# Set-up and projections of the first attention as one unrolled block: composed norms, and the next group's rows and turns during the present group

## The reference

```
def _ln(x, g, b):
    m = jnp.mean(x, -1, keepdims=True)
    v = jnp.var(x, -1, keepdims=True)
    return (x - m) * jax.lax.rsqrt(v + 1e-05) * g + b
...
x = _ln(xx, ln1_g, ln1_b)
...
xn = _ln(x, lnx_g, lnx_b)
yn = _ln(y, lny_g, lny_b)
q = jnp.einsum('bsc,hcd->bhsd', xn, wq)
k = jnp.einsum('btc,hcd->bhtd', yn, wk)
v = jnp.einsum('btc,hcd->bhtd', yn, wv)
```

## Time and profile before

| | |
|---|---|
| time before, median of 3 executions | 2344.16 us (2343.84 to 2350.32) |
| the profiled execution's own time | 2343.02 us |
| its span, first to last instruction | 2341.2 us |
| PE busy, share of the span | 1960.3 us, 84% |
| DVE busy | 1316.7 us, 56% |
| ACT busy | 1011.8 us, 43% |
| POOL busy | 533.9 us, 23% |
| mean granted clock of PE, as a share of full speed | 0.941 |

### The profile page before, as it was taken

How to read it: one execution, slowest core, us unless ns; L and a number is a source line. 1 busy time by engine, 2 the same in 40 slices (tenths; PEclk the granted TensorE clock), 3 DMA queues, 4 the chain that set the end, 5 groups by cost and what they waited for, 6 DMA issues and landing times. The chain is left out here.

```text
span 2341.2 us, 32500 instructions
## 1 busy us (share of the span) xinstructions
PE 1960.3 (84%) x11836; PEld 1237.5 (53%) x11836; DVE 1316.7 (56%) x2301; ACT 1011.8 (43%) x2111; POOL 533.9 (23%) x909
## 2 busy tenths in 40 slices
PE   3778888888799797996999989979999898973695
PEld 1335555555566465663565655535656455442594
DVE  3548888888633597233666632246666343876212
ACT  1238888888622342221656621126565111531121
POOL 2102222222333300332222211022222111131321
PEclk9889999999999899997999999989999999986797
DMA  2243111110000100003000000030000000035395
GB/s 68 72 133 112 40 38 41 40 37 2 1 1 1 54 1 1 1 0 94 1 1 1 1 1 1 0 106 1 1 1 1 1 0 14 1 122 134 115 307 156
DMA packets 99133, 99.60 MB, mean 43 GB/s; under 512 B 33740, under 2 KB 83232, under 8 KB 98848
## 3 DMA queue, kind: packets, MB, share of 16 engines
q1 hardware_dynamic: 95904, 93.21, 13.0%
q0 software_dynamic: 3072, 4.34, 1.0%
HBM read 80.60 MB, written 16.92 MB: 42 GB/s over the span
## 5 line engine op out<-in xcount | busy, mean ns | idle before, releaser
L515 DVE TENSOR_REDUCE negmax<-sps 128x1 f32<-128x1024 f32 x256 | 308.0, 1214 | 21.5 <-PE sps L466 20.8
L559 ACT ACTIVATE prob<-sps,negmax 128x1024 f32<-128x1024 f32 x256 | 286.2, 1118 | 9.2 <-DVE negmax L515 6.5
L475 PE MATMUL sps<-ident,prob 128*128 128x128 f32 x1152 | 178.9, 283 | 55.8 <-ACT prob L559 54.7
L475 PEld LDWEIGHTS sps<-ident,prob 128*128 128x128 f32 x1152 | 131.7, 142 | 144.7 <-ACT prob L559 129.4
L466 PE MATMUL sps<-ks,qs 128*128 128x512 f16 x512 | 162.9, 390 | 22.1 <-DVE ores L535 18.8
L604 POOL TENSOR_TENSOR probT<-probT,after 128x128 f32<-128x128 f32 x256 | 116.5, 455 | 276.8 <-DVE probT L523 192.3
L568 ACT COPY probT<-sps 128x512 f32<-128x512 f32 (+1 forms) x192 | 101.6, 529 | 18.8 <-PE sps L475 18.8
L1313 POOL TENSOR_TENSOR la1qs<-la1qn,la1sin 128x256 f32<-128x256 f32 x64 | 60.3, 971 | 196.7 <-DVE la1qn L1390 196.7
L1313 POOL TENSOR_TENSOR la0qs<-la0qn,la0sin 128x256 f32<-128x256 f32 x64 | 60.3, 971 | 195.6 <-DVE la0qn L1390 195.6
L523 DVE COPY probT<-sps 128x512 f32<-128x512 f32 (+3 forms) x192 | 91.7, 478 | 1.5 <-PE sps L475 1.5
L491 PE MATMUL sps<-probT,vres 128*32 128x128 f32 x2304 | 81.6, 277 | 8.5 <-POOL probT L604 5.7
(11 more groups left out here) (450 smaller groups left out, 4249.2 us busy)
## 6 DMA issues: line engine op xcount, KB each, us to landing
w1e<-in_fc_T SPq DMA_DIRECT2D x16, 1024.0 KB, 5.7
w2e<-in_fc_T SPq DMA_DIRECT2D x16, 1024.0 KB, 8.4
qs<-q_parts SPq DMA_DIRECT2D x128, 64.0 KB, 1.9
ks<-k_parts SPq DMA_DIRECT2D x128, 64.0 KB, 1.9
q_parts<-parts SPq DMA_DIRECT2D x8, 512.0 KB
k_parts<-parts SPq DMA_DIRECT2D x8, 512.0 KB
token_rows<-r_row SPq DMA_DIRECT2D x4, 544.0 KB
mixed<-r_zero SPq DMA_DIRECT2D x1, 2056.0 KB, 10.6
```

What stands on the lines that cost most here:

```text
L475: mm = pe.transpose(slots[n % 4][:, at * P:(at + 1) * P], prob[:, n % 3, t * P:(t + 1) * P], ident[:])
L515: dve.tensor_reduce(negmax[:, n % 4:n % 4 + 1], slots[n % 4][:], X, ALU.max, negate=True).then_inc(s.max_done, 1)
L559: act.activation(prob[:, n % 3, :], slots[n % 4][:], ACT.Exp, bias=negmax[:, n % 4:n % 4 + 1], accum_out=rowsum[:, tile % 2, n % QUAD:n % ...
```

## The change

Both blocks become one, with no loop in it and with more semaphores, so that each step waits for just what it needs.

- The first two norms are composed. With m and v the mean and variance of a row, the doubly normed row is (x - m) / sqrt(v (1 + eps) + eps^2). DVE takes the statistics of x once, writes (x - m) * ln1g (`centre`, L268) and, with the inverse root, times it plus ln1b (`place_x0`, L281) straight to `x0res`. POOL is left with the constants.
- DVE's norm of group g+1 is cut into eight pieces, `norm_piece(g + 1, n)`, one behind each of the eight remainders `low_part(g, n)` (L343) of group g. The third norm is among them.
- PE turns group g+1 (L426) behind the tenth tile of group g; ACT makes its xT and yT there, in a second pair of buffers (the second yT lies in the place of a weight of a later block).
- PE begins a group's q tiles once xT is there (two ACT instructions instead of four), and k and v with yT.
- The copy of v goes from DVE to ACT (L392).
- SP loads the first quarter of x, then `ln1g` and `ln1b`, the four small vectors, the weights one semaphore each, then the rest of x and the gates; it sends q after tile 3 and k after tile 7. DVE begins when the first quarter of x and the two rows are there.
- tanh of the gates (L414) is ACT's last instruction in the block.

The core of the diff, with the old scheduling functions of DVE, ACT and PE left out:

```diff
-        def ln_vector(e, s, n, src, dst, out=None):
...
             with nc.Block() as block:
                 @block.sync
                 def _(sp):
+                    load_x(0)
+                    sp.dma_start(ln1g[:], rows(io["L0_xattn_ln1_g"])).then_inc(s.rows_in, 16)
+                    sp.dma_start(ln1b[:], rows(io["L0_xattn_ln1_b"])).then_inc(s.rows_in, 16)
...
+                    for g in range(1, G):
+                        load_x(g)
...
                     for g in range(G):
                         b, gg = g // (G // B), g % (G // B)
-
-                        sp.wait_ge(s.hi_done, 1 + g * 8 + 8)
-                        sp.wait_ge(s.proj_free_dve, 1 + g * 8 + 8)
                         for t, dst in enumerate((q_parts, k_parts)):
+                            sp.wait_ge(s.hi_done, g * 8 + t * 4 + 4)
+                            sp.wait_ge(s.lo_done, g * 8 + t * 4 + 4)
...
+                    def norm_piece(g, n):
+                        if n == 0:
+                            stats_x(g)
+                        elif n == 1:
+                            moments_x(g)
+                            centre(g, 0)
+                            centre(g, 1)
+                        elif n == 2:
+                            centre(g, 2)
+                            centre(g, 3)
+                            inverse_x(g)
+                        elif n == 3:
+                            place_x0(g, 0)
+                            place_x0(g, 1)
+                        elif n == 4:
+                            place_x0(g, 2)
+                            place_x0(g, 3)
+                        elif n == 5:
+                            stats_x0(g)
+                        elif n == 6:
+                            moments_x0(g)
+                        else:
+                            inverse_x0(g)
+                            normed(g)
...
+                    dve.wait_ge(s.rows_in, 32)
+                    for n in range(8):
+                        norm_piece(0, n)
+                    for g in range(G):
                         for n in range(8):
...
+                            low_part(g, n)
+                            if g + 1 < G:
+                                norm_piece(g + 1, n)
...
+                    for g in range(G):
+                        for n in range(8):
+                            high_part(g, n)
+                            if n == 2 and g + 1 < G:
+                                root_x(g + 1)
+                        if g + 1 < G:
+                            root_x0(g + 1)
+                        value(g, 8)
+                        value(g, 9)
+                        if g + 1 < G:
+                            affine(g + 1)
+                        value(g, 10)
+                        value(g, 11)
+                    act.wait_ge(s.gates_in, 32)
+                    act.activation(gate[:], gate[:], ACT.Tanh).then_inc(s.tanh_done, 1)
...
+                    turn(0)
+                    for g in range(G):
+                        for n in range(12):
+                            project(g, n)
+                            if n == 9 and g + 1 < G:
+                                turn(g + 1)
```

325 lines of the change are left out of this document (169 added, 156 removed).

## The result

| | before | after |
|---|---|---|
| median of 4 executions each, same chip | 2344.55 us (2343.84 to 2350.32) | 2286.23 us (2284.53 to 2287.81) |
| ratio, 95% interval | | 0.9747 (0.9735 to 0.9759) |
| the profiled execution's own time | 2343.02 us | 2286.99 us |
| its span | 2341.2 us | 2285.2 us |
| first matmul of the attention | 164.31 us | 108.28 us |

The change saves 58.3 us between the medians, where 50.4 were forecast. The expected things happened: no group boundary with a wait, a start 22.65 us earlier, and PE's clock up from the end of the first q tiles to the block's end. What was wrong are sizes, nearly all to the same side.

A forecast was written before the change was run, and what follows sets the result against it. PE was taken to bound the block before the attention, losing time to start, boundaries and clock. Savings 19.4 + 26.2 + 5.7 less 0.6 and 0.3 lost gave 50.4 us, a median of 2293.8, range 2288 to 2302.

The forecast's parts named there:

- What bounds the stretch: Block before the attention: PE's matmuls fill 82.3 of 161 us; the rest is start, boundaries and clock.
- the first load: Before DVE's first instruction: quarter of x and two rows there at 8.3 us instead of 13.01, saving 4.7.
- The chain to the first projection: From DVE's first instruction to PE's first projection: 13.2 us instead of 27.86.
- The boundaries: Between PE's groups: only transposes stay, three boundaries cost 3.0 us and not 29.2, saving 26.2.
- a late `h`: At the group boundaries: DVE's `h` level with PE, no margin; 0.2 us a boundary, 0.6 lost.
- The rival of a late DVE: DVE late at every group boundary, 2.2 us each: 2300, or 2307 if the clock falls too; chance 0.17.
- The clock: PE's q tiles: clock stays up after the first group's ramp; 2.7 of 8.4 us lost remain, 5.7 saved.
- the clock stayed low: Rival: PE's unbroken run of 192 f32 instructions stays at the low clock, 79.6 us later, 2373; chance 0.02.
- The end: Block's end: ACT is last, 3.6 us from PE's end to the attention's first matmul, 0.3 lost.
- The table switch: Rival: switching costs a drain, 1.4 us more at the first root and at the block's end, 2296.6; chance 0.08.
- The stated range: For the median: own range 2289 to 2298 us, widened to 2288 to 2302 for drain and late DVE.
- The clock behind the barrier: At the attention's start: clock's state uncertain by 2 us either way, as a ramp cost 1.5 to 2.7.

The follow-up runs named there:

- e3: Changed kernel with the third norm (pieces 5 to 7), the turn and xT of the next group behind the present group's last tile; ratio 0.9879.
- e5: Kernel before the change with only the first two norms composed into one; ratio 0.9983, attention starts at 160.58 us.
- e4: Changed kernel with the four small vectors' transfers issued ahead of ln1g and ln1b; ratio 0.9773, attention starts at 111.52 us.
- e7: Changed kernel with three more DVE statistics instructions, results unread, for each of a group's four tiles; ratio 0.9823.
- e10: Changed kernel with tanh of the gates moved behind ACT's third high part of the last group; ratio 0.9743, PE's stop 1.56 us.
- e6: Changed kernel with four extra ACT instructions ahead of tanh, stretching PE's stop at the block's end to 5.03 us; ratio 0.9760.
- e13: Changed kernel with one small ACT copy ahead of tanh's table load; one execution, PE's stop 3.24 us, first heads 12.77 us.
- e16: Changed kernel with one small ACT copy ahead of tanh's table load, repeated; one execution, PE's stop 3.24 us, first heads 12.75 us.
- e17: Changed kernel with three small ACT copies ahead of tanh's table load; one execution, PE's stop 3.58 us, first heads 12.74 us.
- e1: Changed kernel with PE turning the next group behind the twelfth tile instead of the tenth; ratio 0.9766, attention starts at 114.97 us.
- e2: Changed kernel with one buffer each for xT and yT, the turns still behind the tenth tile; ratio 0.9779.
- e18: Changed kernel with the turn behind the twelfth tile, run again; one execution, attention starts at 114.53 us, first heads 12.11 us.
- e8: Changed kernel with 72 transposes of the identity on PE ahead of the first turn; ratio 0.9754, attention starts at 108.25 us.
- e12: Changed kernel with early tanh, finer start, and 96 identity transposes on PE ahead of the first turn and 12 behind it; ratio 0.9726.
- e15: Changed kernel with early tanh and finer start, without identity transposes; ratio 0.9732, attention starts at 104.23 us.

## Why the prediction was wrong, point by point

**What bounds the stretch** was right. e3 brings the boundary back by its two waits and the clock; e5, which takes a norm and nothing else, gains at the start alone.

**The step that failed** is the first load. It was put as "The two rows, 2 x 131 KB spread to 128 partitions, ran at 93 GB/s in their window, thus 2.8 us more, 7.4", which with 0.9 for the signal "gives 8.3". DVE began at 5.77: 2.5 of the surplus, and even the low end of 7.0 was too high. The window's rate was read as a property of the transfer. The row had a sign against it: its DMA share is 0.68, where the windows at 320 GB/s and more show 1.01 to 1.05. In e4 the slow rate comes back with the vectors ahead of the rows, and goes with them. By itself this step would have left the time in the range (2293.8 less 2.5 is 2291.3); it is the largest of several that add up.

**The chain to the first projection** took 18.22 - 5.77 = 12.45 and not 13.2 (0.75 more). The links show less than was summed: the statistics and moments 1.60 from start to next start instead of 1.93, as moments now follow without a gap (5.77 + 1.40 to 7.09), and the third norm with the step to PE 3.70 (10.96 to 14.66) instead of 3.89 + 0.14. The rest is 0.09 in the placing and 0.06 of rounding (the terms give 13.14), against 0.08 more in the centring.

**The boundaries** cost 0.87 each instead of 1.0 (0.4 more), and the 0.6 for a late `h` was not lost: no turn has a wait. `h` stood ready 0.4 ahead, and e7 puts the whole margin at 1.0 us. The rival of a late DVE, 2300, did not come about.

**The clock** stayed up after the first group, as forecast, and its ramp cost 1.8 where 2.7 had been kept (0.9 more). This term is luck: in the other traces the ramp was 1.5 to 2.8, with the same code up to it in most, so that 2.7 could have come as well. That the clock stayed low (2373) did not come about.

**The end** was 3.07 and not 3.6 (0.5 more): 0.94 between ACT's last instruction and the next matmul, where 1.5 of the 1.65 had been taken.

**The table switch.** The rival put 1.4 us more at the root and at the end. The root stands 0.01 behind its load's end (7.54 + 1.28 to 8.83), tanh 0.02 (105.84 + 1.28 to 107.14), in e10 0.02 as well. The Trainium skill (ScalarE: Activation LUTs, What ACT_TABLE_LOAD costs) has about 1283 ns for the load, which these rows confirm at 1283 ns in the groups by line, and about 1380 ns of drain on top, which no row of this case shows. The rival fell by the rows.

These six (load, chain, ramp, boundaries, late `h`, end) are 2.5 + 0.75 + 0.9 + 0.4 + 0.6 + 0.5 = 5.65, and 50.4 + 5.65 is the 56.0 at the attention's start. The stated range gave the chain and the ramp no room, and the load only 1.3 downwards; all its own low ends together reach 2288.9 (and the high ones 2299.3, not 2298).

**The clock behind the barrier** gives the next 1.8, the gain in the first heads. The text had it, "the clock's state at the start of the attention (2 either way)", within its own range, but at zero in the sum. What decides it is only half settled. Stops of 3.24 us and more lost it in six traces of six (before, e5, e6, e13, e16, e17), 1.56 kept it in three of three; 3.07 kept it in five of ten, lost part of it in three (10.79), and lost it in two. The changed kernel kept it twice and e1's kernel lost it twice, but two pairs that agree do not rule out chance. The ramp, too, differs between traces with the same code ahead of it. What decides at 3.07 stays open.

The last 0.6 within the later attention, and the experts' stage, in which the two profiles differ by over 2 us against the sign of the gain, were not looked into by an experiment.

Three of the sizes were off to the same side because the unknown was priced from a row in which something else was included: the load with vectors ahead, the moments with a gap, the barrier with a transfer.

## What to carry to other kernels

A rate read from a window belongs to all that was in the queue then. Before it prices another transfer, see what stood ahead; and issue what the first instruction needs ahead of the small scattered pieces, here for 3.4 us.

Removing a wait in the middle of a busy stretch pays twice where the clock falls in it: at each boundary here 8.9 us in waits and slow transposes and another 1.9 on average in slow matmuls behind it. The norm ahead is worth most of it (e3); the early turn and the second buffer guard one and the same wait, and without either of them 5.4 to 5.6 us come back (e1, e2).

A last instruction behind a table load belongs into an idle time earlier in the block: 1.5 us here.

## What the runs showed of the hardware

- Stops of 1.54 and 1.60 us between busy stretches at full clock did not lower the granted clock at any of nine boundaries (e1, e2, e18). A stop of 2.73 left it up at two boundaries and lost it behind the third (e7). One of 2.97 followed by 1.60 lost it (e8), and one of 3.74 followed by 1.54 did so three times (e3). At the block's end 3.07 went both ways, and after 3.24 and more the clock was down or fell soon.
- With the vectors of 4-byte pieces ahead, the loads behind them passed at 91 to 116 GB/s (e4), against 320 to 371 without them ahead.
- Between the last engine's end and the next block's first matmul lay 0.94 us, a barrier included, where no transfer was awaited.
- Transposes of the identity alone bring the clock up: in e12 the q tiles behind 96 of them take 7.03 us and not 8.87. As built this gained 0.4 us (e12 against e15), and nothing with two stops behind them (e8).
